# Softmax reciprocals broadcast by DMA instead of by selector products, in an AdaLN attention and MLP kernel

## The reference

```
h = layernorm(x) * (1 + ca) + sa
q = rope(h @ Wq) (16 heads of 64);  k = rope(h @ Wk), v = h @ Wv (4 heads of 64, each shared by 4 query heads)
attn = softmax(q @ k.T * 64**-0.5);  o = attn @ v;  x = x + ga * (o @ Wo + bo)
h = layernorm(x) * (1 + cb) + sb
x = x + gb * (gelu(h @ bin(w1).T + b1) @ bin(w2).T + b2)        bin(w) = mean(|w|) per row * sign(w)
```

## Time and profile before

| | |
|---|---|
| median of 3 runs | 700.21 us (699.74 to 702.76) |
| the profiled execution | 700.25 us; its span, first to last instruction, is 698.5 us |
| PE busy | 668.9 us (96%) |
| ACT, DVE, POOL busy | 551.4, 516.5, 430.1 us |
| DMA | 24.75 MB, mean 35 GB/s |
| steady steps | 12 steps from 93.8 to 546.5 us |

### The profile page before, as it was taken

One profiled execution on the slowest core, in us unless ns is written; L12 is line 12 of the kernel. 1 busy time (PEld: TensorE's weight loads), 2 busy tenths in 40 slices (PEclk: granted clock), 3 DMA queues, 4 the chain that ended last, 5 costly groups with the idle time before them and its releaser, 6 DMA issues.

```text
span 698.5 us, 13530 instructions
## 1 busy us (share of the span) xinstructions
PE 668.9 (96%) x3733; PEld 519.5 (74%) x3733; DVE 516.5 (74%) x1196; ACT 551.4 (79%) x1149; POOL 430.1 (62%) x397
## 2 busy tenths in 40 slices
PE   4698999999999999999999999999999999998897
PEld 3566787877777787878787777778787878667786
DVE  6566777778788777777787778887777877778762
ACT  4478887888787888878887878787887888768676
POOL 1657685857686776768585768577676758543110
PEclk9699999999999999999999999999999999999999
DMA  8111111011111111111102111111111110200111
GB/s 241 31 32 33 33 26 39 18 38 28 32 31 32 32 20 29 32 32 32 31 16 43 20 32 31 32 32 28 26 27 33 32 34 18 48 17 3 39 39 46
DMA packets 31580, 24.75 MB, mean 35 GB/s; under 512 B 16688, under 2 KB 26944, under 8 KB 31552
## 3 DMA queue, kind: packets, MB, share of 16 engines
q1 hardware_dynamic: 31552, 24.40, 16.6%
HBM read 4.47 MB, written 2.10 MB: 9 GB/s over the span
## 4 chain that ended last, share of the span: by engine, by line
PE 90%; DVE 3%; ACT 3%; POOL 1%; issue 1%; DMA 0%; SPq 0%; POOLq 0%; DVEq 0%
PE o_ps L1021 15%; PE o_ps L1011 11%; PE unit_ps L957 9%; PE score_ps L992 8%; PE unit_ps L946 8%; PE score_ps L994 8%; PE unit_ps L973 8%; PE o_ps L1078 4%; PE unit_ps L931 3%; PE unit_ps L932 3%; PE unit_ps L933 3%; PE unit_ps L967 2%; PE unit_ps L961 2%; PE unit_ps L1055 1%; PE unit_ps L1056 1%
## 5 line engine op out<-in xcount | busy, mean ns | idle before, releaser
L521 POOL TENSOR_TENSOR probs_lo<-probs,probs_hi 128x512 fp32r<-128x512 f32 x160 | 202.1, 1283 | 67.7 <-ACT probs_hi L662 67.6
L772 DVE TENSOR_REDUCE w_all<-unit_ps 128x2 f32<-128x512 f32 x256 | 166.2, 685 | 52.4 <-PE unit_ps L957 50.9
L659 ACT ACTIVATE probs<-score_ps 128x512 f32<-128x512 f32 x256 | 150.6, 589 | 21.2 <-PE score_ps L994 18.6
L507 POOL TENSOR_TENSOR rot_sum<-rot_a,rot_b 128x512 f32<-128x512 f32 (+1 forms) x96 | 104.7, 1097 | 99.3 <-DVE rot_b L764 99.0
L511 POOL TENSOR_TENSOR qk_rot<-rot_sum,qk_rot 128x512 fp32r<-128x512 f32 (+1 forms) x96 | 105.0, 1101 | 36.3 <-ACT qk_rot L609 36.3
L957 PEld LDWEIGHTS unit_ps<-k_hi,q_hilo 128*128 128x128 f32 x512 | 88.7, 191 | 41.3 <-issue 17.9
L957 PE MATMUL unit_ps<-k_hi,q_hilo 128*128 128x256 f32 x512 | 118.3, 318 | 0.7 <-ACT q_hilo L591 0.4
L946 PEld LDWEIGHTS unit_ps<-ident_r,qk_rot 128*128 128x128 f32 x640 | 101.9, 194 | 17.7 <-issue 4.3
L946 PE MATMUL unit_ps<-ident_r,qk_rot 128*128 128x128 f32 x640 | 110.2, 264 | 4.6 <-POOL qk_rot L511 3.8
L992 PE MATMUL score_ps<-q_hilo,k_hi 128*128 128x512 f32 x256 | 112.9, 441 | 1.1 <-DMA q_him<-neg_max_t 1.1
L777 DVE TENSOR_TENSOR o_t<-o_un,unit_ps 64x256 f32<-64x256 f32 x248 | 103.5, 417 | 4.4
(11 more groups left out here) (120 smaller groups left out, 1123.4 us busy)
## 6 DMA issues: line engine op xcount, KB each, us to landing
q_him<-q_hilo SPq DMA_DIRECT2D x64, 256.0 KB
out_x<-w_all SPq DMA_DIRECT2D x16, 128.0 KB, 1.8
xa<-in_L_attn_x SPq DMA_DIRECT2D x3, 640.0 KB, 7.5
q_him<-neg_max_t SPq DMA_DIRECT2D x64, 4.0 KB
w_all<-in_L_attn_Wq SPq DMA_DIRECT2D x1, 512.0 KB, 5.3
w_sb<-in_L_ffn_w SPq DMA_DIRECT2D x2, 256.0 KB, 3.0
wo_sb<-in_L_attn_Wo SPq DMA_DIRECT2D x1, 512.0 KB, 8.2
sums<-o_un SPq DMA_DIRECT2D x32, 8.0 KB, 2.0
```

The lines of the kernel that those rows point to most:

```text
L507: pool.tensor_tensor(total, rot_a[k % 2][:, 0:heads, :], rot_b[k % 2][:, 0:heads, :], ALU.add).then_inc(rot_summed, 1)
L521: pool.tensor_tensor(probs_lo[s % 2][:, jc, :, :], probs[s % 2][:, jc, :, :], probs_hi[s % 2][:, jc, :, :].bitcast(F32), ALU.subtract).the ...
L659: ins = act.activation(probs[s % 2][:, jc, :, :].rearrange("p h i -> p (h i)"), score_ps[jc][:, :], ACT.Exp, scale=SCALE)
L772: dve.tensor_reduce(neg_max[u[1] // 4][:, first:first + C], ps[:, :].rearrange("p (c j) -> p c j", c=C), AX.X, ALU.max, negate=True).then_ ...
```

## The change

The selector products `bc` go, and with them `select`, `recip_parts` and the split of the reciprocals. `o_un` becomes 128 partitions high, laid out by half, head and pair. For each half of the heads SP now does five transfers instead of three:

1. `gather_sums` as before, 8 KB;
2. `second_heads`: the second heads of four pairs move from partitions 0 to 63 to partitions 64 to 127, 256 KB (this overwrites the row of sums, so it waits for transfer 1);
3. `reciprocals_to_row`: 8 KB of reciprocals to one row, in partition 96 (half 0) or 97 (half 1), after DVE's reciprocal;
4. and 5. `reciprocals_to_all`: after the row has landed, two transfers that each read 4 KB of that row 64 times and write 64 partitions of `o_t`, 256 KB each.

Then DVE multiplies two pairs at once (128 partitions by 512, both operands in SBUF), the words `mul0` to `mul3`. The first of each half waits for transfers 2, 4 and 5. `SLOTS` is a new order of the same other words. In it `recip0` stands at the end of slot 5 and `mul0` in slot 0 of the next step; `recip1` stands at the start of slot 2 and `mul2` in slot 3.

```
-    "S0 s4 s5 m s6 m s7 xT0 xT0 m m S1 m qt4 qt4 m mT1 qt4 qt4",
-    "S0 m s8 S1 m qkv02 qt5 qt5 qt5 qt5 qkv12 m m m m",
-    "S0 s9 m recip1 s10 qt6 qt6 qt6 qt6 m S1 s11 m m m m qkv00 mT2",
-    "qkv10 S0 m s12 m m S1 bc4 bc5 qt7 qt7 qt7 qt7 m bc6 m m s13",
-    "S0 bc7 S1 m s14 m s15 kt0 m kt0 stats kt0 rstd kt0 kt1 norm m m kt1 kt1 kt1 m mT3 yT0",
-    "S0 qkv01 m m S1 m qt0 yT1 recip0 qt0 m qt0 m qt0 m",
-    "qt1 S0 qt1 qt1 qt1 s0 qt2 qt2 S1 qt2 s1 qt2 m s2 m s3 m zT0 zT0 m m m qkv11 mT0",
-    "S0 S1 bc0 m bc1 bc2 m m qt3 qt3 qt3 qt3 m m bc3 m",
+    "s4 S0 s5 s6 m S1 m s7 mul0 xT0 xT0 mul1 m m m m",
+    "S0 qt4 qt4 qt4 mT1 m qt4 qkv02 qkv12 m qt5 S1 qt5 qt5 qt5 m m m s8 m",
+    "S0 recip1 S1 m s9 qt6 qt6 qt6 qt6 m m s10 s11 m qkv00 qkv10 m mT2 m",
+    "S0 s12 s13 S1 kt0 kt0 m qt7 mul2 qt7 qt7 qt7 m m mul3 m kt0 m kt0 m",
+    "S0 m s14 m kt1 m s15 kt1 S1 kt1 m kt1 m m yT0 mT3",
+    "stats S0 yT1 m qt0 qt0 m m qkv01 qt0 qt0 S1 m qt1 m qt1 zT0 zT0 qt1 qt1 recip0 m",
+    "S0 rstd m s0 S1 s1 s2 m s3 m m qkv11 qt2 qt2 qt2 qt2 m mT0 m",
+    "qt3 S0 S1 m m m m m qt3 qt3 norm qt3 m",
...
-OUT_UNITS = [("bc", s) for s in range(4, PAIRS)] + [("yT", 0), ("yT", 1), ("zT", 0)]
+LATE_UNITS = ([("qt", s) for s in range(4, PAIRS)] + [("s", h) for h in range(4, HEADS)] + [("mT", q) for q in range(1, 4)])
+OUT_UNITS = [("yT", 0), ("yT", 1), ("zT", 0)]
...
-TAIL_AT = {("bc", 4): 5, ("bc", 5): 5, ("bc", 6): 6, ("bc", 7): 6, ("yT", 0): 7, ("yT", 1): 8, ("zT", 0): 9}
+TAIL_PRODUCTS_AT = 6
+TAIL_AT = {("yT", 0): 7, ("yT", 1): 8, ("zT", 0): 9}
...
-        q_him = [sb(f"q_him{i}", [DH + 1, 4, N], F32R) for i in range(2)]
+        q_him_all = sb("q_him_all", [P, 8, N], F32R)
+        q_him = [q_him_all[:, 4 * i:4 * i + 4, :] for i in range(2)]
+        recip_rows = [q_him_all[96 + i:97 + i, :, :].bitcast(F32) for i in range(2)]
...
-        o_un = sb("o_un", [DH + 1, PAIRS, 2, N])
+        o_un = sb("o_un", [P, 2, 2, 4, N])
...
-                sp.dma_start(sums[:, :], o_un[DH:DH + 1, 4 * half:4 * half + 4, :, :]
-                             .rearrange("o s h (b t) -> o (s h b) t", t=16)).then_inc(sums_in[half], 16)
-            def spread_reciprocals(st, half, batch):
-                sp.wait_ge(recip_lo_ready, st.count(2, half + 1, batch))
-                for first, part in ((0, recip_hi), (32, recip_lo)):
-                    sp.dma_start(recip_parts[half][first:first + PAIRS, :].bitcast(F32).rearrange("h (b t) -> h b t", t=16),
-                                 part[:, :].bitcast(F32)).then_inc(recip_in[half], 16)
+                sp.dma_start(sums[:, :], o_un[DH:DH + 1, half, :, :, :]
+                             .rearrange("o h s (b t) -> o (h s b) t", t=16)).then_inc(sums_in[half], 16)
+            def second_heads(st, half, batch):
+                sp.wait_ge(sums_in[half], st.count(16, 16, batch))
+                sp.dma_start(o_un[DH:P, half, 0, :, :].rearrange("p s i -> p (s i)"),
+                             o_un[0:DH, half, 1, :, :].rearrange("p s i -> p (s i)")).then_inc(second_in[half], 16)
+            def reciprocals_to_row(st, half, batch):
+                sp.wait_ge(recip_ready, st.count(2, half + 1, batch))
+                sp.dma_start(recip_rows[half][:, :, :].rearrange("o h (b t) -> o (h b) t", t=16),
+                             recip[:, :]).then_inc(rows_in[half], 16)
+            def reciprocals_to_all(st, half, batch):
+                sp.wait_ge(rows_in[half], st.count(16, 16, batch))
+                if half == 0 and not st.prep:
+                    sp.wait_ge(z_ready, B - 1)
+                for h in range(2):
+                    sp.dma_start(o_t[h * DH:h * DH + DH, 4 * half:4 * half + 4, :].rearrange("p s i -> p (s i)"),
+                                 recip_rows[half][:, 4 * h:4 * h + 4, :].rearrange("o s i -> o (s i)").unsqueeze(1).broadcast_to([1, DH, 4 * N])).then_inc(recip_in[half], 16)
...
-                    spread_reciprocals(st, 1, -1)
+                    second_heads(st, 1, -1)
+                    reciprocals_to_row(st, 1, -1)
+                    reciprocals_to_all(st, 1, -1)
                 if st.attn:
                     maxima(st, 2, 0)
                     high_parts(st, 3, 0)
                     maxima(st, 3, 0)
                     gather_sums(st, 0, 0)
-                    spread_reciprocals(st, 0, 0)
+                    second_heads(st, 0, 0)
+                    reciprocals_to_row(st, 0, 0)
                 if st.prep:
                     high_parts(st, 0, 1)
+                if st.attn:
+                    reciprocals_to_all(st, 0, 0)
+                if st.prep:
                     maxima(st, 0, 1)
                     high_parts(st, 1, 1)
...
+                            pair = (s - 2) % 8
+                            if st.number != 0 and pair < 4:
+                                act.wait_ge(o_t_ready, st.count(4, pair // 2 + 1, -1))
+                            act.activation(o_un[0:DH + 1, pair // 4, :, pair % 4, :],
+                                           o_ps[s % 2][0:DH + 1, :].rearrange("p (h i) -> p h i", h=2),
...
-                if kind == "bc":
-                    for h in range(2):
-                        ins = dve.tensor_tensor(o_t[h * DH:h * DH + DH, u[1], :], o_un[0:DH, u[1], h, :],
-                                                ps[h * DH:h * DH + DH, 0:N], ALU.mult)
-                    ins.then_inc(o_t_ready, 1)
...
-                dve.wait_ge(recip_ready, st.count(2, half + 1, batch))
-                dve.tensor_copy(recip_hi[:, :], recip[:, :]).then_inc(recip_hi_ready, 1)
-                dve.wait_ge(recip_hi_ready, st.count(2, half + 1, batch))
-                dve.tensor_tensor(recip_lo[:, :], recip[:, :], recip_hi[:, :].bitcast(F32),
-                                  ALU.subtract).then_inc(recip_lo_ready, 1)
+            def normalise_heads(st, quarter, batch):
+                half, two = quarter // 2, slice(2 * quarter, 2 * quarter + 2)
+                own = slice(quarter % 2 * 2, quarter % 2 * 2 + 2)
+                if quarter % 2 == 0:
+                    dve.wait_ge(second_in[half], st.count(16, 16, batch))
+                    dve.wait_ge(recip_in[half], st.count(32, 32, batch))
+                dve.tensor_tensor(o_t[:, two, :], o_un[:, half, 0, own, :], o_t[:, two, :], ALU.mult).then_inc(o_t_ready, 1)
...
-                if kind == "bc":
-                    half = u[1] // 4
-                    if u[1] % 4 == 0:
-                        pe.wait_ge(recip_in[half], st.count(32, 32, ahead(u)))
-                    ins = pe.matmul(ps[:, 0:N], select[:, 2 * (u[1] % 4):2 * (u[1] % 4) + 2, :].rearrange("k h d -> k (h d)"),
-                                    recip_parts[half][:, :], start=True, stop=True)
```

More of the change, by code:

```diff
@@ L85, in parsed @@
                 product += 1
-            elif kind in ("stats", "rstd", "norm", "recip"):
+            elif kind in ("stats", "rstd", "norm", "recip", "mul"):
                 slot.append((kind, int(number or 0)))
@@ L210, in slot_parts @@
         parts = [("part", u, part, part == PARTS[u[0]] - 1) for _, u in units(st, s) for part in range(PARTS[u[0]])]
-        return [("recip", 1)] * (s == TAIL_RECIPROCALS_AT) + parts
+        return ([("recip", 1)] * (s == TAIL_RECIPROCALS_AT)
+                + [("mul", 2), ("mul", 3)] * (s == TAIL_PRODUCTS_AT) + parts)
     held = {"scores": st.attn, "pv": st.attn if s >= 1 else st.out, "un": st.attn if s >= 2 else st.out,
-            "stats": st.norm, "rstd": st.norm, "norm": st.norm}
+            "stats": st.norm, "rstd": st.norm, "norm": st.norm, "recip": (st.attn, st.out), "mul": (st.out,) * 4}
     return [w for w in ORDER[s]
-            if (not st.tail and has(st, w[1]) if w[0] == "part" else not st.tail and (st.attn, st.out)[w[1]] if w[0] == "recip"
+            if (not st.tail and has(st, w[1]) if w[0] == "part" else held[w[0]][w[1]] and not (st.tail and s > 1 - w[1] // 2) if w[0] in ("recip", "mul")
                 else held[w[0]])]
@@ L387, in adaln_layer @@
         pool_lo_ready = sem("pool_lo_ready")
-        o_un_ready, recip_ready, recip_hi_ready, recip_lo_ready, o_t_ready = (
-            sem("o_un_ready"), sem("recip_ready"), sem("recip_hi_ready"), sem("recip_lo_ready"), sem("o_t_ready"))
+        o_un_ready, recip_ready, o_t_ready = sem("o_un_ready"), sem("recip_ready"), sem("o_t_ready")
         sums_in = [sem(f"sums_in{i}") for i in range(2)]
+        second_in = [sem(f"second_in{i}") for i in range(2)]
+        rows_in = [sem(f"rows_in{i}") for i in range(2)]
         recip_in = [sem(f"recip_in{i}") for i in range(2)]
@@ L553, in _ @@
             act.activation(ident_r[:, :], ident[:, :], ACT.Copy).then_inc(ident_r_ready, 1)
-            for half in range(2):
-                act.activation(select[32 * half:32 * half + 32, :, :],
-                               ident[0:32, 0:PAIRS].unsqueeze(2).broadcast_to([32, PAIRS, DH]), ACT.Copy).then_inc(select_ready, 1)
             act.wait_ge(wkv_in, 16)
@@ L566, in unit @@
```

(19 more changed lines are left out.)

16 lines of the change are left out of this document (5 added, 11 removed).

## The result

The changed kernel takes 1278.55 us (median of 4 runs, 1275.65 to 1281.78) against 701.39 for the kernel before beside it (699.74 to 702.76). The ratio is 1.823, 95% interval 1.816 to 1.830. The prediction said 1222 us in a range of 850 to 1450. The profiled execution has a span of 1275.8 us.

The account below looks back on a forecast made before the run. PE was taken as the bound, busy for 668.9 of 698.5 us. The sum was 700.2 - 15 (removed products) + 465 (stalls) + 72 (slow clock) = 1222 us, in a range of 850 to 1450.

Parts of the forecast that it names:

- Removed: On PE, eight selector products a batch at 0.12 us go: 0.94 us a step, 15.0 us over the kernel.
- B = 9.4 us: Packet time of one 256 KB broadcast read from one partition, at 28 GB/s, the middle of 16 and 41.
- Who waits: DVE waits at `mul0` and `mul2`, PE sooner at `S0` of slots 0 and 4, its maxima queued behind the broadcasts.
- The stalls, 465 us: PE waits 14.6 us for each half, 438 us over 15 steps; with two tail stalls, about 15 and 12, 465.
- The clock, 72 us (53 to 93): After each of 31 stalls TensorE restarts at half clock, losing 1.7 to 3.0 us, 2.3 taken: 72 us.
- (a): Broadcasts run like any 256 KB transfer, 1.5 us each, and are hidden; only removed products count: 685 us; chance 0.14.
- (b): Each broadcast's packets take 2.1 to 6.4 us because long pieces are served better: 700 to 1030 us; chance 0.05.
- (c): New slot order brings maxima 1 us late to `S0` in slot 2, 15 steps: 700 us; chance 0.03 with (d).
- (d): On PE, other stalls fill the selector products' time, so it does not come back: 700 us; chance 0.03 with (c).
- DVE: DVE's work falls from 29.15 to about 23.7 us a step, covered by PE before and after, worth nothing.
- the bound of 4.3 us more: On DVE, four products with both operands in SBUF may wait for POOL, up to 4.3 us more a step.

Follow-up runs that it names:

- the wide source: The changed kernel, but both broadcasts read 64 partitions of `wo_sb` instead of the one row, so attention output is wrongly scaled: 685.78 us, ratio 0.979.
- the row in device memory: The changed kernel, but the row of reciprocals is kept in device memory instead of partition 96 or 97; computes the whole layer: 685.82 us, ratio 0.979.
- the exchange in SP's list: The changed kernel with the maxima of quarter 2 and of the next batch's quarter 0 issued ahead of the broadcasts: 1240.86 us, ratio 1.771.
- the variant with one slow broadcast: The changed kernel with only the second broadcast of each half reading 64 partitions of the output weights: 994.45 us, ratio 1.417.

## Why the prediction was right

The sign, the mechanism and the size were right. Each term by its own step:

**Removed.** 15.0 us for 128 selector products. With the wide source and with the row in device memory the kernel takes 685.8 us, 15.4 below the 701.15 beside it. PE bounds it again (36.12 of 36.84 us a step). That the sum is so close has some luck: PE's busy time fell by 23.4 us and its idle time rose by 6.9 (29.6 to 36.5). Why the busy time fell by more than the products' price isn't shown.

**B = 9.4 us.** Measured 9.7, 27 GB/s. That the middle of two far rows came so near was luck. The lower row (16 GB/s, short pieces) was a bound as argued. The upper one, 41 GB/s for 4 KB of maxima, was a burst: 64 KB into one row ran at 26 GB/s, so writes are no faster than reads here. The sentence by the table of the Trainium skill named above gave 9.6.

**Who waits.** PE at `S0` of slots 0 and 4 with DVE at `mul0` and `mul2`: seen in every step, and the exchange in SP's list confirmed that the maxima held PE.

**The stalls, 465 us.** Half 0 was 15.4 to 16.1 us instead of 14.6, half 1 17.1 to 18.0, 493 us for the thirty instead of 438. In half 1 the row took 3.3 us from its issue to the broadcasts' (about 3 assumed, counted from the reciprocal, which starts 0.9 us earlier), the two broadcasts 21.0 to DVE (20.1 by B = 9.4), and PE had 8.1 us of work, not 8.5. In the tail two stalls took 31.5 us (27 predicted), both in front of MLP products behind DVE. At the first DVE stood at `mul0`; at the second it stood in front of the MLP's result and waited for a store of `out` that SP had issued behind the last two broadcasts, and not at `mul2`:

```profile
1207.48 1.13 SPq L461 DMA_DIRECT2D o_t<-q_him_all  x2
1208.98 64.95 SPq L495 DMA_DIRECT2D out_x<-w_all  x16
1228.78 0.42 DVE L864 TENSOR_TENSOR w_all<-score_ps,xa 128x256 f32<-128x256 f32 x1 [17.07 <-DMA out_x<-w_all]
```

Set against the variant with the row in device memory, which has the same 3605 instructions on PE, PE is idle for 1275.8 - 725.2 = 550.6 us instead of 682.0 - 645.5 = 36.5: the waiting costs 514 us, a tenth more than predicted.

**The clock, 72 us (53 to 93).** By the same comparison PE's busy time grew by 725.2 - 645.5 = 79.7 us, 2.5 for each of 32 stalls (the prediction took 2.3 for 31, though its own sum has 30 and two in the tail). Restart and recovery look as in the earlier trace rows, in order of time on PE:

```profile
610.93 0.63 PE L1004 MATMUL score_ps<-q_hilo,k_hi 128*128 128x512 f32 x1
611.36 0.63 PE L1006 MATMUL score_ps<-q_him_all,k_lo 65*128 65x512 f32 x1
611.78 0.49 PE L1033 MATMUL o_ps<-probs_hi,v_hi 128*65 128x512 f32 x1
```

The starts lie 0.43 us apart until 611.78, 3.1 us after the restart at 608.63; after 644.88 it is 4.4 us. These are short ones. After the restart at 681.40 the clock is still at half 5.6 us later:

```profile
686.00:687.00 1.00, 1.00 (x4) 0.51 (x3) 0.93 (x2) 0.67 (x2) 0.00 (x0) 0.50 0.00 0
```

Over the 32 restarts the granted clock came back after 3.0 to 6.6 us, 5.3 on average, and 46% of 5.3 is 2.4 us. In the variant with one slow broadcast the average was 4.6. The two terms, 514.1 + 79.7 = 593.8 us, are the difference of the spans by construction, since idle and busy time add up to a span; the medians differ by 592.7.

**The rivals.** (a) was a true account of another kernel: with a source of 64 partitions it gives 685, as worked out. (b) is excluded by B. (c) and (d) cost nothing that shows in the time. Without slow broadcasts the new order does have a wait of its own, at the scores of slot 4 and not at slot 2, where (c) put it: up to 0.9 us a step and 1.4 in the last, 8.1 us in all with the row in device memory. PE's busy time fell by enough to cover it.

**DVE.** Predicted 23.7 us a step, 23.64 in the window; with POOL at work beside it (the row in device memory) 25.64, within the bound of 4.3 us more.

## What to carry to other kernels

A broadcast is no faster than the ways that its source reaches allow, however many its destination has: 256 KB out of one partition took 9.7 us, out of 64 partitions 1.4, and out of one row in device memory they landed 0.5 us after the latter. Before replacing a product by a transfer, take the PE work between the last input and the first use (8 us here) and lay it beside the transfer chain, and look at what else stands in line behind that transfer: the engine that stopped first was waiting for 4 KB that had nothing to do with it. And a queue walks in order: moving a small issue ahead of a large one moves its wait and its issue ahead too, which made the good variant 23 us slower, because it had nothing to spare at the next use.

## What the hardware showed that I had not expected

- SP's issues behind the two broadcasts took 6.35 and 9.49 us instead of 0.7 and 0.5: the issuing engine itself stood still for 16 us. The second ended at 641.05, 3.7 us before DVE had the broadcasts, so it did not wait for them to land; what it waited for isn't shown.
- Two broadcasts from two issuing engines out of partitions 96 and 100, which do not share a way by the table of the Trainium skill named above, took 18.4 us together, SP's landing at 11.1 as if alone. They ran almost one after the other, so a second queue gained little: 18.4 us for 512 KB against 20.8 out of one partition.
- Neighbouring partitions are slow as a destination too: 64 KB into partitions 0 to 3 took 3.95 us, into 0, 4, 8 and 12 2.5.
- A stall of 7 to 9 us costs nearly as much in clock as one of 15 to 17: 67.7 / 32 = 2.1 us against 79.7 / 32 = 2.5.
